# A two-layer state-space, mixture and attention kernel: other states turned by TensorE, in both halves, and the step-size bias as a weight row

## The reference

```
dtr, Bm, Cm = jnp.split(xdbl, [DT_RANK, DT_RANK + D_STATE], axis=-1)
dt = jax.nn.softplus(jnp.einsum('blr,dr->bld', dtr, Wdt) + bdt)
def step(h, ins):
    dt_t, u_t, B_t, C_t = ins
    h = jnp.exp(dt_t[..., None] * A) * h + (dt_t * u_t)[..., None] * B_t[:, None, :]
    y_t = jnp.einsum('bdn,bn->bd', h, C_t)
```

## Time and profile before

| | |
|---|---|
| median of 3 runs | 864.05 us |
| profiled execution, its own time | 863.14 us |
| its span, first to last instruction | 860.6 us |
| mean granted TensorE clock | 0.897 of full |
| busy: PE, DVE, ACT, POOL | 80%, 68%, 70%, 49% |
| first and last state's first scan | 121.6 and 575.8 us |
| share of the DMA engines' time | 32% |

### The profile page before, as it was taken

One profiled execution on the slowest core, in us unless ns is written; L12 is line 12 of the kernel. 1 busy time (PEld: TensorE's weight loads), 2 busy tenths in 40 slices (PEclk: granted clock), 3 DMA queues, 4 the chain that ended last, 5 costly groups with the idle time before them and its releaser, 6 DMA issues.

```text
span 860.6 us, 13106 instructions
## 1 busy us (share of the span) xinstructions
PE 688.3 (80%) x4227; PEld 482.5 (56%) x4227; DVE 584.9 (68%) x851; ACT 601.6 (70%) x1235; POOL 417.7 (49%) x359
## 2 busy tenths in 40 slices
PE   5799956797886877977768675768797888888886
PEld 5588835575674565655636645767683333334433
DVE  6335669897997987979878868796325455545542
ACT  3444559878888888789887987774645667765663
POOL 4300058797896987978968778770000000000000
PEclk8889979799797997999987967889999999999998
DMA  3224525454453553644634436710200000000000
GB/s 108 99 66 132 179 100 169 135 166 144 135 186 111 156 170 119 182 137 147 189 100 142 164 109 175 249 60 1 74 26 1 1 1 1 1 1 1 13 14 24
DMA packets 48130, 85.78 MB, mean 100 GB/s; under 512 B 6320, under 2 KB 11448, under 8 KB 48064
## 3 DMA queue, kind: packets, MB, share of 16 engines
q1 hardware_dynamic: 48064, 84.96, 31.6%
HBM read 83.37 MB, written 1.57 MB: 99 GB/s over the span
## 4 chain that ended last, share of the span: by engine, by line
PE 34%; ACT 26%; issue 14%; DVE 10%; POOL 1%; DVEq 0%; POOLq 0%; ACTq 0%
ACT scaled L777 6%; ACT ps L761 5%; PE ps L1621 4%; ACT decay_sb L761 3%; PE ps L1570 3%; PE ps L1911 3%; PE ps L1880 2%; PE ps L1601 2%; PE ps L1888 2%; DVE ps L1074 2%; PE ps L1919 2%; PE ps L1615 2%; PE ps L1821 1%; DVE moe L1074 1%; DVE hc L1082 1%
## 5 line engine op out<-in xcount | busy, mean ns | idle before, releaser
L567 POOL TENSOR_TENSOR drive<-dtu,b_sb 128x512 f32<-128x512 f32 x160 | 203.3, 1278 | 0.7
L575 POOL TENSOR_TENSOR hc<-moe,c_sb 128x512 f32<-128x512 f32 x128 | 166.0, 1297 | 42.8 <-DVE moe L1074 42.2
L1074 DVE TENSOR_TENSOR_SCAN moe<-ps,drive 128x512 f32<-128x512 f32 x128 | 153.3, 1198 | 0.2
L1621 PEld LDWEIGHTS ps<-ident,hc 128*128 128x128 f32 x1024 | 133.2, 157 | 32.4 <-issue 27.4
L1621 PE MATMUL ps<-ident,hc 128*128 128x128 f32 x1024 | 150.7, 299 | 0.0
L1074 DVE TENSOR_TENSOR_SCAN ps<-decay_sb,ps 128x512 f32<-128x512 f32 x96 | 117.5, 1224 | 39.5 <-PE ps L1601 22.7
L981 ACT ACTIVATE probs<-ps 128x1024 f32<-128x1024 f32 (+1 forms) x96 | 87.8, 916 | 74.3 <-PE ps L1888 64.2
L1601 PE MATMUL ps<-ident,scaled 128*128 128x128 f32 x384 | 68.7, 308 | 71.3 <-ACT scaled L777 69.0
L777 ACT ACTIVATE scaled<-dtuT,bT 128x128 f32<-128x128 f32 x384 | 121.4, 389 | 0.0
L761 ACT ACTIVATE ps<-dt,negA 128x510 f32<-128x510 f32 x160 | 105.9, 676 | 1.8 <-DVE ps L1086 1.2
L580 POOL TENSOR_TENSOR stat<-stat,halfc 128x4 f32<-128x4 f32 x7 | 7.0, 1007 | 201.0 <-DVE stat L1297 201.0
(11 more groups left out here) (257 smaller groups left out, 1208.0 us busy)
## 6 DMA issues: line engine op xcount, KB each, us to landing
b_sb<-bc_rows SPq DMA_DIRECT2D x128, 256.0 KB, 3.2
c_sb<-bc_rows SPq DMA_DIRECT2D x128, 256.0 KB, 3.3
wbuf<-in_pack SPq DMA_DIRECT2D x16, 514.0 KB, 3.4
wbuf<-in_pack SPq DMA_DIRECT2D x8, 512.0 KB, 4.0
x_sb<-in_x SPq DMA_DIRECT2D x4, 256.0 KB, 3.5
out<-x_sb SPq DMA_DIRECT2D x4, 256.0 KB, 2.3
w_in<-in_w_in SPq DMA_DIRECT2D x1, 512.0 KB
bc_rows<-bcx SPq DMA_DIRECT2D x8, 64.0 KB, 2.9
```

The lines of the kernel that those rows point to most:

```text
L567: pool.tensor_tensor(drive_of(N, half), dtu[:, N // STATES % 2, half], b_sb[:, N % B_RING], ALU.mult) \
L575: pool.tensor_tensor(hc[:, 2 * (N % DEEP) + half], h_of(q), c_sb[:, N % C_RING], ALU.mult).then_inc(sem["hc_pooled"], 1)
L1074: dve.tensor_tensor_scan(h_of(q)[:, turn], decay_bank(q)[:, turn], source[:, turn], 0.0, ALU.mult, ALU.add).then_inc(sem["scan_done"], 1)
L1621: last = pe.matmul(ps[:, Y_BANK + half, block], hc[:, 2 * (N % DEEP) + half, block], ident[:], start=False, stop=True, is_transpose=True, ...
```

## The change

- Turned are now states 1, 3, 6, 8, 11 and 14 of each group, in both halves (`TURNED_AT`); the other ten are pooled in both halves. Steps t turn both halves of dtu into `dtuT` (now a part of `xm`), 256 channels wide; `scaled` is one buffer of four blocks of 256 columns, where it was two of 512 in all. PE turns half 0 ahead of the state, half 1 at its start, into the other of the two banks, from which the scan of half 1 reads.
- In a turned state DVE does the product with C of half 0 between the two scans; a first scan behind a turned state waits for that state's second scan.
- POOL's drives follow a table (`DRIVE_PLAN`, ring of 6). B rows are loaded for pooled states only: 80 in place of 128.
- The bias of dt: a ninth row of the step-size weights against a row of ones in `bcx`. POOL puts the bias column into `row` (`bias_row`), PE makes the nine rows of both directions in a new step v ahead of x of group 0, ACT copies them. Relu goes; DVE takes the maximum with 0 in the addition.

```diff
@@ -124,8 +124,8 @@
-    tensor = {1: "T11", 2: "T12", 3: "T13", 4: "x0", 5: "b0", 14: "dt00", 15: "dt01"}
-    others = {1: "T11", 2: "T12", 3: "T13", 4: "x0", 5: "b0", 10: "setup"}
+    tensor = {1: "T11", 2: "T12", 3: "T13", 4: "v0 x0", 5: "b0", 14: "dt00", 15: "dt01"}
+    others = {1: "T11", 2: "T12", 3: "T13", 4: "v0 x0", 5: "b0", 10: "setup"}
...
@@ -136,8 +136,8 @@
-    readers += events("dt01 zero t0")
-    order += events("t0")
+    readers += events("dt01 zero t00 t01")
+    order += events("t00 t01")
...
@@ -147,7 +147,7 @@
-                          11: [("dt", n, 0)], 13: [("dt", n, 1)], 14: [("b", n)], 15: [("t", n)]})
+                          11: [("dt", n, 0)], 13: [("dt", n, 1)], 14: [("t", n, 0), ("b", n)], 15: [("t", n, 1)]})
...
@@ -257,35 +257,59 @@
+TURNED_AT = (1, 3, 6, 8, 11, 14)
+POOLED_STATES = STATES - len(TURNED_AT)
 def turned(N):
-    return N % 4 != 0
+    return N % STATES in TURNED_AT
 def turned_before(N):
-    return N - (N + 3) // 4
+    return len(TURNED_AT) * (N // STATES) + sum(j < N % STATES for j in TURNED_AT)
 def pooled_drive(q):
-    return q % HALVES == 1 or not turned(q // HALVES)
+    return not turned(q // HALVES)
 def drives_before(q):
...
-    return 2 * N - turned_before(N) + (half and not turned(N))
+    return q - HALVES * turned_before(N) - (half if turned(N) else 0)
...
+DRIVE_RING = 6
 def decay_before(q):
...
+def drive_plan():
+    issued, plan = 0, []
+    for e in range(ALL):
+        room = sum(POOLED[max(i - DRIVE_RING, 0)] < HALVES * e for i in range(DRIVE_RING, len(POOLED))) + DRIVE_RING
+        group, j = divmod(e, STATES)
+        known = HALVES * POOLED_STATES * (group + (2 if j >= STATES - 2 else 1))
+        needed = drives_before(HALVES * min(e + 2, ALL))
+        until = max(needed, min(issued + 2, room, known, len(POOLED)))
+        assert until <= min(known, room)
+        plan.append(POOLED[issued:until])
+        issued = until
+    assert issued == len(POOLED)
+    return plan
+DRIVE_PLAN = drive_plan()
...
@@ -338,8 +362,9 @@
-        bcx = sb("bcx", [XROWS, COLS])
-        dtuT = sb("dtuT", [P, COLS])
+        bcx = sb("bcx", [XROWS + 1, COLS])
+        row = sb("row", [P, 2 * HALVES, RANK + 1])
+        dtuT = xm[:, 4:12].rearrange("p t d -> p (t d)").rearrange("p (t c) -> p t c", c=INNER)
...
@@ -366,9 +391,9 @@
-        drive = sb("drive", [P, DRIVES + 2, COLS])
+        drive = sb("drive", [P, DRIVE_RING, COLS])
...
-        scaled = sb("scaled", [P, 2, COLS])
+        scaled = sb("scaled", [P, 4, INNER])
...
@@ -441,7 +466,10 @@
         def drive_of(N, half):
-            return drive[:, N % DRIVES] if half else drive[:, DRIVES + N // 4 % 2]
+            return drive[:, drives_before(HALVES * N + half) % DRIVE_RING]
+        def turned_bank(N, half):
+            return ps[:, H_BANKS[(N + half) % OWN_H]]
...
@@ -490,9 +518,10 @@
             def load_b(N):
-                after(sp, "drive_ready", drives_before(HALVES * max(N - B_RING + 1, 0)))
-                sp.dma_start(b_sb[:, N % B_RING], bc_rows[N // STATES, N % STATES].partition_broadcast(P)) \
-                    .then_inc(sem[f"b_loaded{N % B_RING}"], 16)
+                n = N - turned_before(N)
+                after(sp, "drive_ready", HALVES * (n - B_RING + 1))
+                sp.dma_start(b_sb[:, n % B_RING], bc_rows[N // STATES, N % STATES].partition_broadcast(P)) \
+                    .then_inc(sem[f"b_loaded{n % B_RING}"], 16)
...
@@ -516,7 +545,8 @@
-                load_b(N)
+                if not turned(N):
+                    load_b(N)
...
@@ -538,6 +568,15 @@
+            pool.memset(row[:], 0.0).then_inc(sem["row_zeroed"], 1)
+            pool.memset(bcx[:], 1.0).then_inc(sem["row_zeroed"], 1)
+            def bias_row():
+                pool.wait_ge(sem["row_zeroed"], 2)
+                pool.wait_ge(sem["consts_loaded"], 48)
+                pool.tensor_copy(row[:, :, RANK:RANK + 1].rearrange("p (d h) n -> p d h n", d=2),
+                                 par[:, :, :, TAPS + 1:TAPS + 2]).then_inc(sem["row_ready"], 1)
...
@@ -562,9 +601,12 @@
             def drive_half(N, half):
-                pool.wait_ge(sem[f"b_loaded{N % B_RING}"], 16 * (N // B_RING + 1))
-                after(pool, "scan_done", 2 * (N - (DRIVES if half else 8)) + half + 1)
-                pool.tensor_tensor(drive_of(N, half), dtu[:, N // STATES % 2, half], b_sb[:, N % B_RING], ALU.mult) \
+                n = N - turned_before(N)
+                pool.wait_ge(sem[f"b_loaded{n % B_RING}"], 16 * (n // B_RING + 1))
+                i = drives_before(HALVES * N + half) - DRIVE_RING
+                if i >= 0:
+                    pool.wait_ge(sem["scan_done"], POOLED[i] + 1)
+                pool.tensor_tensor(drive_of(N, half), dtu[:, N // STATES % 2, half], b_sb[:, n % B_RING], ALU.mult) \
...
@@ -617,22 +661,14 @@
                 elif ev[0] == "state":
...
-                    if N == 0:
-                        pool.wait_ge(sem["dtu_ready"], HALVES)
-                        for first in range(DRIVES - 1):
-                            for half in range(HALVES):
-                                if half or first and not turned(first):
-                                    drive_half(first, half)
-                    M = N + DRIVES - 1
-                    if M < ALL:
-                        if M % STATES == 0:
-                            pool.wait_ge(sem["dtu_ready"], HALVES * (M // STATES + 1))
-                        if not turned(M):
-                            drive_half(M, 0)
-                    if N:
+                    for n, q in enumerate(DRIVE_PLAN[N]):
+                        if n == 1 and N:
+                            times_c(N - 1, 1)
+                        if q:
+                            pool.wait_ge(sem["dtu_ready"], HALVES * (q // HALVES // STATES + 1))
+                            drive_half(*divmod(q, HALVES))
+                    if N and len(DRIVE_PLAN[N]) < 2:
...
-                    if M < ALL:
-                        drive_half(M, 1)
...
@@ -714,25 +750,27 @@
+                elif kind == "v":
+                    act.activation(w_dt[DT_ROW:XROWS + 1].rearrange("p d c -> p (d c)"), ps[DT_ROW:XROWS + 1, SIDE_BANK], ACT.Copy) \
+                        .then_inc(sem["side_free"], 1)
...
                 elif kind == "t":
-                    act.activation(dtuT[:], side, ACT.Copy).then_inc(sem["side_free"], 1)
+                    act.activation(dtuT[:, :, half * P:half * P + P], side.rearrange("p (t c) -> p t c", c=P), ACT.Copy).then_inc(sem["side_free"], 1)
                 elif kind == "x":
...
-                    act.activation(bcx[:], ps[0:XROWS, SIDE_BANK], ACT.Copy).then_inc(sem["side_free"], 1)
+                    act.wait_ge(sem["row_zeroed"], 2)
+                    act.activation(bcx[0:XROWS], ps[0:XROWS, SIDE_BANK], ACT.Copy).then_inc(sem["side_free"], 1)
                 else:
...
-                    bias = par[:, dr, half, TAPS + 1:TAPS + 2]
...
-                    act.activation(dt_a[:], bank, ACT.Abs, bias=bias).then_inc(sem["dt_abs"], 1)
+                    act.activation(dt_a[:], bank, ACT.Abs).then_inc(sem["dt_abs"], 1)
...
-                    act.activation(bank, bank, ACT.Relu, bias=bias).then_inc(sem["dt_relu"], 1)
...
@@ -769,12 +807,11 @@
-                act.wait_ge(sem["side_free"], SIDE["t", g] + 1)
+                act.wait_ge(sem["side_free"], SIDE["t", g, 1] + 1)
...
-                after(act, "drive_turned", n - 1)
+                after(act, "drive_turned", HALVES * n)
...
-                    block = slice(t * P, (t + 1) * P)
-                    last = act.activation(scaled[:, n % 2, block], dtuT[:, block], ACT.Copy, scale=bT[:, t, j:j + 1])
+                    last = act.activation(scaled[:, t], dtuT[:, t], ACT.Copy, scale=bT[:, t, j:j + 1])
...
@@ -1053,23 +1090,24 @@
-                    dve.wait_ge(sem["dt_relu"], HALVES * g + half + 1)
-                    dve.tensor_tensor(dt[:, g % 2, half], dt_a[:], dt_bank(g, half), ALU.add).then_inc(sem["side_free"], 1)
+                    dve.scalar_tensor_tensor(out=dt[:, g % 2, half], in0=dt_bank(g, half), scalar=0.0, in1=dt_a[:],
+                                             op0=ALU.max, op1=ALU.add).then_inc(sem["side_free"], 1)
             def scan(N, half):
...
-                if half:
-                    dve.wait_ge(sem["drive_ready"], drives_before(q + 1))
-                    after(dve, "hc_pooled", shared_before(q) - 1)
-                    source = drive_of(N, 1)
-                elif turned(N):
-                    dve.wait_ge(sem["drive_turned"], turned_before(N) + 1)
-                    source = h_of(q)
+                if turned(N):
+                    dve.wait_ge(sem["drive_turned"], HALVES * turned_before(N) + half + 1)
+                    source = turned_bank(N, half)
                 else:
...
+                    source = drive_of(N, half)
+                if half:
+                    after(dve, "hc_pooled", shared_before(q) - 1)
```

(42 more changed lines are left out.)

16 lines of the change are left out of this document (9 added, 7 removed).

## The result

The changed kernel takes 890.55 us (median of 4 runs, 888.5 to 892.75) against 864.65 us (862.56 to 867.24) for the kernel before on the same chip: **ratio 1.0309, interval 1.0285 to 1.0333, slower by 26 us.** The forecast was 877 us, 857 to 888: the direction is right, the size is half of what came, and the range misses it.

A forecast was written before the change was run, and what follows sets the result against it. DVE was taken to set the pace in the states, PE to have no idle time in the expert stretch. States +6.7, in front +5.1 and +1.8 make 13.6 us on 863.14: 876.7, rounded 877, range 857 to 888.

The forecast's parts named there:

- The terms for the groups: 128 states: groups 1 to 4 +3.6 us, group 0 +0.5, groups 5 and 6 +0.9, last group +0.8; summed as +6.7.
- rival A: States: ACT's relief reaches DVE and shortens each group's waits by 5.1 us: 844 us, 857 if half arrives; chance 0.14.
- The b loads fall from 128 to 80: Loads of 256 KB: nobody waits for one, so fewer could only help; no time was added.
- the last group's +0.8: Last group of states: it has no projections, its links cost 1.4 us and little is won, +0.8 us.
- The expert stretch, +5.1: PE's queue ahead of x: v's passes 2.2 us, stall behind POOL's bias row 2.1, ACT's copy 0.8; bounds 2.2 and 9.
- rival C: PE's queue: more stalls bring the 1.2 GHz clock, v, x and turns take twice as long: 5 to 12 us, 885; 0.20.
- The links, +1.4 a group: DVE in turned states: each op waiting for the one before costs 0.12 us, 12 a group, 11.5 us over 96.
- Rival B: DVE in turned states: links are free, a linked scan starts as soon as an unlinked one: 865 us; chance 0.13.
- The waits, 8.0 to 7.5 a group: DVE's waits per group: 0.45 + 3.6 + 1.15 + 0.2 + 0.1 + 1.0 + 1.0 = 7.5 us against 8.0 before.
- State 10: DVE's wait there: now pooled, scan 1.25 us after ACT's copy starts, so the wait falls from 2.31 to 1.15 us.
- The start, +1.8: Start of the states: ACT's first decays stand behind t of both halves, at 122.7 and not 120.9, +1.8 us.
- The assumption on ACT: ACT in turned states: a 256-column scaled pass takes 0.40 us, near the Gelu, about 1.6 us a state.

The follow-up runs named there:

- e9: Changed kernel with SP issuing the rows of B of pooled states, and the store before a group's rows, two states earlier: 880.36 us, ratio 1.0210.
- e13: Kernel before with the B rows, and the store ahead of them, issued two states earlier in SP's queue: 863.27 us, ratio 1.0006.
- e4: Changed kernel with POOL putting the bias into its rows ahead of the expert pairs, v staying ahead of x: 886.11 us, ratio 1.0256.
- e1: Changed kernel with DVE doing both scans of a turned state before the product with C, as before: 891.55 us, ratio 1.0301.
- e2: Kernel before with the product with C between the two scans in turned states, 96 links of the first kind: 867.74 us, ratio 1.0057.
- e8: Changed kernel with states 1, 3, 5, 10, 12 and 14 turned instead of 1, 3, 6, 8, 11 and 14: 905.85 us, ratio 1.0503.
- e12: Changed kernel with v ahead of the experts, B rows two states earlier, layer-1 loads spread, only states 1, 3, 11, 14 turned: 873.00 us, ratio 1.0094.
- e14: e12 with six turned states kept in the last group and ACT's first decays ahead of its second copy of dtu: 869.10 us, ratio 1.0067.
- e17: Kernel before with the ninth weight row in place of Relu, step v ahead of u: 858.36 us, ratio 0.9950.
- e15: Kernel before with the ninth weight row only, step v behind z ahead of the expert stretch: 861.62 us, ratio 0.9989.

## Why the prediction was wrong

It said slower with 0.68, and most of its mechanisms are in the trace. The sum was too small, at these steps:

- **An error of adding.** The terms for the groups, 3.6 + 0.5 + 0.9 + 0.8, make 5.8 us and not the 6.7 that stands in the sum; all terms together make 12.7 us, not 13.6. The price of half of rival A, 857, halves the links together with the relief; with the links in full it is 862.
- **"The b loads fall from 128 to 80; nobody waits for one, and if that cover were gone it could only help", and the last group's +0.8.** This is the step that failed. The last group became 8.2 us longer. The loads are fewer, but POOL now asks for them earlier, ahead of its products, while SP still issues them behind C rows that wait for those products. Fewer transfers do not mean earlier ones. The same edit of SP's queue takes 7.6 us off the last group of the changed kernel (e9, ratio 1.0210 for 1.0309) and gains nothing before (e13). By itself it brings the time, 880.4 us, into the stated range.
- **The expert stretch, +5.1.** Stall and copy were right to 0.1 us; the stretch grew by 8.5. v's sixteen passes took 2.75 us for the 2.2 estimated, and x and the down product ran at the lower clock, about 2.8 us. That was rival C's mechanism, given 0.20 and priced at 5 to 12 us over everything; it belonged into the term itself, whose bounds of 2.2 and 9 did hold 8.5. e4 adds that the stall was not what lowered the clock.
- **The links, +1.4 a group, 11.5 in all.** Right in kind and somewhat small: the first kind costs 0.15 us, the second 0.22, not 0.12 each; own time grew by 2.0 us a group, 15.8 in all, of which 12.8 are gone without the links (e1). Rival B (links are free, 0.13) is refuted by e2: 1.0057, interval 1.0034 to 1.0080, from links alone. With it falls, for scans of 512 columns in this kernel, what the Trainium skill says (VectorE: DVE Perf Modes, "The DRAIN you can't avoid"), that a semaphore between chained DVE operations adds nothing.
- **The waits, 8.0 to 7.5 a group.** Of groups 1 to 4 they were 7.35 on the mean before and after. State 8: 3.6 forecast, 3.0 measured; state 6: 0.45, and 0.41; state 14: 1.0, and 1.2; state 2: 1.0, and 0.4. State 10: 1.15, and 1.9, a reading that failed: copy at 324.17 plus 1.25 is 325.42, only 0.20 ahead of the old scan at 325.62, so the forecast's own rows give 2.1. It was 2.2 in three of the four groups, with x at 3.74 us (3.59 before), and 0.96 in group 3, where x took 2.48. Rival A (the relief reaches DVE, 0.14) had it wrong, and e8 and e12 show under what condition it would hold: only with no turned state behind the copies of y does the wait at state 8 fall, and then to 1.62.
- **The start, +1.8**: as forecast. e14, with the decays ahead, won the wait back (2.27 for 4.07) and lost 1.2 us at state 1.

The assumption on ACT was right: four scaled passes of 256 columns take 1.59 us from start to start, 0.40 each, as these rows show against the earlier trace rows:

```profile
130.28 1.69 ACT L814 ACTIVATE scaled<-xm,bT 128x256 f32<-128x256 f32 x4
131.87 1.32 ACT L799 ACTIVATE decay_sb<-dt,negA 128x510 f32<-128x510 f32 x2
```

The Trainium skill's 93 ns of access overhead (Perfetto Trace Analysis, "Optimizing Scalar/DVE Operations") would have made it 2.0 us; the trace has 0.19 us saved by each fusion, twice that. The section adds that a profiled latency is about twice its figure, with half of it overlapping the next instruction; here the whole 0.19 us lies between the starts.

In one sum: 26.5 us = 15.9 (states) + 8.5 (expert stretch) + 1.8 (start) + 3.3 (behind the states, mostly the clock) - 2.1 (an earlier arrival at the expert stretch) - 0.8 (outside the span), to a rounding of 0.1. Against the 12.7 us that the forecast's terms make: +7.4 in the last group (8.2 for 0.8), +4.4 in groups 1 to 4 (8.0 for 3.6), +3.4 in the expert stretch, +3.3 behind the states, -1.7 in group 0 (-1.2 for +0.5), nothing in groups 5 and 6 (0.9, as forecast), and the -2.1 and -0.8.

## What to carry to other kernels

When an order is changed so that one engine works further ahead, follow what it needs back into the queue that issues it: a load that stands behind transfers waiting for this same engine's later work closes a cycle, and having fewer loads does not open it. Before counting on the relief of an engine, divide the pacing engine's time into own time and waits: here 39 us less on ACT changed the waits by nothing, while DVE's own time grew by 16 us, 13 of them by a reordering, and that reordering could not be undone without giving PE too little time. A small step put into a full PE queue costs more than its passes: price its copy and what runs at the lower clock behind it, and put it where the engine has gaps.

## What the runs showed of the hardware

- A DVE scan or product that waits for the instruction directly before it starts later than one that doesn't: a product behind its scan by 0.14 us (1.26 for 1.12), a scan behind a scan whose source it overwrites by 0.22 us (1.35 for 1.13).
- TensorE's granted clock fell to the 1.2 GHz level behind v, sixteen passes on 8 or 128 rows and 9 columns, busy without a gap, and 0.68 us of waiting: x took 3.57 us with no stall ahead of v and 3.74 with 2.09 us of it, for 1.88 without v. In e17, with v elsewhere, the six passes of the first taps behind it took 3.77 us for 2.72 in e15.
- What follows the last state takes 280 to 287 us, by granted clock, in executions of kernels that do the same work there. Most of the spread lies in the last products into y, 9.7 to 15.3 us from the last scan to the addition; the remainder took 271.4 to 274.2 us in nineteen executions and 277.1 in one (e15). One profiled execution does not tell a few us of such a kernel; e14's took 862.98 us, the median of its runs 869.10.
